# Block products of a recurrence summed two chunks at a time in 32x32 tiles of TensorE, with the projections issued in quarters

## The reference

```python
xa = _ln(x, ln1_w, ln1_b)
sx = shift(xa) - xa
mw, mk, mv, mr, mg = low-rank mixes of xa + sx * maa_x
w = exp(-exp(time_decay + tanh(xw @ decay_w1) @ decay_w2))
r, k, v = xr @ Wr.T, xk @ Wk.T, xv @ Wv.T        # 32 heads of 16
g = silu(xg @ Wg.T)
def step(s, inp):                                # s: 16 x 16 per head
    a = k_l[..., :, None] * v_l[..., None, :]
    out = einsum('bhs,bhst->bht', r_l, faaaa * a + s)
    return a + w_l[..., None] * s, out
y = group_norm(outs) * gn_w + gn_b
x = x + y * g @ Wo.T
rr = sigmoid(xr2 @ fWr.T); kk = square(relu(xk2 @ fWk.T))
x = x + rr * (kk @ fWv.T)
```

## Time and profile before

| | |
|---|---|
| median of 3 runs | 921.98 us (920.86 to 922.21) |
| profiled execution, its own time | 921.95 us |
| its span | 919.9 us |
| PE busy | 870.7 us, 6490 records |
| DVE busy | 639.5 us |
| ACT busy | 352.8 us |
| POOL busy | 294.9 us |

### The profile page before, as it was taken

How to read it: one execution, slowest core, us unless ns; L and a number is a source line. 1 busy time by engine, 2 the same in 40 slices (tenths; PEclk the granted TensorE clock), 3 DMA queues, 4 the chain that set the end, 5 groups by cost and what they waited for, 6 DMA issues and landing times.

```text
span 919.9 us, 16352 instructions
## 1 busy us (share of the span) xinstructions
PE 870.7 (95%) x6490; PEld 585.2 (64%) x6490; DVE 639.5 (70%) x1110; ACT 352.8 (38%) x715; POOL 294.9 (32%) x281
## 2 busy tenths in 40 slices
PE   7699999799999999999998999999999999999997
PEld 5477568457764686557764676646865577457674
DVE  3357966898479836997379954898468965986341
ACT  1222145523553146423363243531464236316422
POOL 3033641374107520373105720175202730640000
PEclk9799999899999999999999999999999999999999
DMA  8820102000010001100021000200001000000010
GB/s 309 307 69 0 47 20 75 1 1 1 2 69 24 1 2 60 56 1 1 2 70 47 1 1 2 93 23 1 2 24 46 1 1 2 24 24 2 1 46 23
DMA packets 17020, 34.09 MB, mean 37 GB/s; under 512 B 2224, under 2 KB 3888, under 8 KB 16944
## 3 DMA queue, kind: packets, MB, share of 16 engines
q1 hardware_dynamic: 14048, 31.20, 9.5%
q10 hardware_dynamic: 2896, 1.84, 0.6%
HBM read 24.65 MB, written 8.39 MB: 36 GB/s over the span
## 4 chain that ended last, share of the span: by engine, by line
PE 65%; DVE 17%; issue 5%; POOL 5%; ACT 4%; DMA 2%; SPq 1%; DVEq 0%; POOLq 0%; ACTq 0%
PE PB L496 21%; PE PC L502 8%; PE CH L578 6%; PE PC L496 6%; POOL prod L1953 3%; PE CH L637 3%; PE CH L614 3%; PE PC L671 3%; PE PA L489 3%; DVE av L1550 2%; PE PB L371 2%; DVE RA L1520 2%; DMA sq_Wo<-in_square 2%; DVE xmix L1458 2%; DVE wprod L1505 2%
## 5 line engine op out<-in xcount | busy, mean ns | idle before, releaser
L1943 POOL TENSOR_TENSOR xmix<-xmix,xa 128x512 f32<-128x512 f32 x80 | 96.5, 1227 | 190.9 <-DVE xmix L1458 190.9
L578 PE MATMUL CH<-prod,ones 128*128 128x512 f32 x272 | 143.3, 627 | 14.6 <-DVE prod L1482 5.2
L1953 POOL TENSOR_TENSOR prod<-RA,K 128x512 f32<-128x512 f32 x112 | 132.3, 1196 | 68.2 <-DVE RA L1520 41.0
L1458 DVE SCALAR_TENSOR_TENSOR xmix<-PA,chan,sx 128x256 f32<-128x256 f32 x160 | 66.1, 475 | 47.9 <-PE PA L489 47.9
L578 PEld LDWEIGHTS CH<-prod,ones 128*128 128x128 f32 x272 | 47.2, 194 | 64.9 <-issue 35.9
L1550 DVE TENSOR_TENSOR av<-CH,vT 128x512 f32<-128x512 f32 x112 | 76.2, 681 | 14.2 <-PE CH L578 14.0
L1132 ACT ACTIVATE st<-av,half 32x512 f32<-32x512 f32 x64 | 74.6, 1166 | 20.9 <-DVE av L1595 19.5
L1556 DVE TENSOR_REDUCE yred<-av 128x64 f32<-128x512 f32 (+2 forms) x112 | 76.9, 686 | 3.9
L496 PE MATMUL PC<-sqb,sq_fWk 128*128 128x256 f32 x256 | 58.6, 383 | 2.4 <-DVE sqb L1674 2.4
L496 PE MATMUL PB<-xmix,sq_Wg 128*128 128x256 f32 x256 | 58.5, 382 | 0.0
L496 PE MATMUL PB<-xmix,sq_Wr 128*128 128x256 f32 x256 | 58.5, 383 | 0.0
(11 more groups left out here) (162 smaller groups left out, 1407.2 us busy)
## 6 DMA issues: line engine op xcount, KB each, us to landing
x<-x_rows SPq DMA_DIRECT2D x11, 512.0 KB, 3.3
x<-in_x SPq DMA_DIRECT2D x8, 512.0 KB, 3.9
x_rows<-x SPq DMA_DIRECT2D x8, 512.0 KB, 3.4
out_x<-x SPq DMA_DIRECT2D x8, 512.0 KB, 2.7
ctx_t<-in_ctx SPq DMA_DIRECT2D x5, 512.0 KB, 4.9
y<-in_ctx SPq DMA_DIRECT2D x3, 512.0 KB, 8.1
sq_Wk<-in_square SPq DMA_DIRECT2D x1, 1024.0 KB, 13.1
sq_Wv<-in_square SPq DMA_DIRECT2D x1, 1024.0 KB, 16.4
```

Of the source, the lines that this page charges most:

```text
L578: pe.matmul(CH[:, (g % 2) * CHUNK:(g % 2 + 1) * CHUNK], ones16[:], prod[:, g % 3, :], start=True, stop=True).then_inc(chunk_mm, 1)
L1458: i = dve.scalar_tensor_tensor(xmix[:, SLOT_OF[name], ct, :], PA[:, ct * L:(ct + 1) * L], vec("maa_" + name, ct), sx[:, ct, :], ALU.add, A ...
L1943: pool.tensor_tensor(m, m, xa[:, ct:ct + 2, 1:L + 1], ALU.add).then_inc(mix_ready, 1)
L1953: pool.tensor_tensor(by_pair(prod[:, g % 3, :], h), r, k, ALU.mult).then_inc(prod_pool, 1)
```

## The change

**Pairs of chunks in tiles.** The chunks are visited in pairs (`VISITS`: 0 and 1, then 2 alone, then 3 and 4, and so on to 15 and 16). `ones16` is zero outside its 32x32 blocks on the diagonal too, so a sum needs only tiles (q, q) of the array: 32 partitions in, 32 out. The new code runs the first chunk of a pair on the four tiles (q, q) and the second on the four tiles (q, q+1), so that its sums land one quadrant (32 partitions) further: eight matmuls of 512 columns instead of two. The lone chunk is cut in two halves of 256 columns for the two sets. Since the second chunk's sums are shifted, the values they are weighed with have to be shifted too: the columns of Wv are rolled by 32 for that half of the channels at the start (on the host, as a layout of the weights), and the turns of v and of the sum `yint` use an identity of 160 columns that shifts back. Chunks are renumbered so that the halves of a pair lie in different halves of the channels.

**Waits.** PE waits for both products of a pair and for all weighings of the pair before it. `prod` has four buffers instead of three. DVE does both weighings of a pair, then both reductions. `D` (block decays) moves from `yred` to `prod`, and ACT's `b_block_decay` waits for `wprod_ready` instead of `yint_ready`.

**Quarters and order.** `a_phi_g` comes in two parts, and `a_key`, `a_value`, `a_receptance`, `a_gate`, `c_wo`, `c_key`, `c_receptance` and `c_value` in four quarters. The lists of all five queues are written anew.

```diff
-    CHUNKS = [(0, c) for c in range(DIAG)] + [(h, c) for h in INTRA for c in range(h)]
+
+    CHUNKS = [(0, 0), (0, 1), (1, 0)] + [(h, c + two * h // 2) for h in INTRA[1:] for c in range(h // 2) for two in range(2)]
     N_CHUNKS = len(CHUNKS)
+    VISITS = [(0, 2), (2, 3)] + [(g, g + 2) for g in range(3, N_CHUNKS, 2)]
...
-        ident = sb("ident", [P, P])
+        ident = sb("ident", [P, P + 32])
...
-        D = [yred[:, 0:L], yred[:, L:2 * L], prod[:, 2, 0:L], prod[:, 2, L:2 * L]]
+        D = [prod[:, 2 + ct // 2, (ct % 2) * L:(ct % 2 + 1) * L] for ct in range(CT)]
...
+        def chunk_sums(g):
+
+            h, c = CHUNKS[g]
+            lo = CHUNK // 2 if h == 1 else CHUNK * (c // max(h // 2, 1))
+            return CH[:, lo:lo + CHUNK]
...
+            def turn_values(values, t):
+
+                for ct in range(CT):
+                    lo = 32 * (ct // 2)
+                    mm = pe.matmul(CH[:, t * C + ct * P:t * C + (ct + 1) * P], values[:, ct * L + t * P:ct * L + (t + 1) * P],
+                                   ident[:, lo:lo + P], start=(ct == 0), stop=False, is_transpose=True, skip_group_check=True)
+                return mm
...
+            def columns_tile(out, mt, w, rhs, signal):
                 for kt in range(CT):
+                    mm = pe.matmul(out[:, mt * L:(mt + 1) * L], w[:, kt, mt * P:(mt + 1) * P], rhs[:, kt, :],
+                                   start=(kt == 0), stop=(kt == CT - 1))
+                if mt % 2:
+                    mm.then_inc(signal, 1)
+
...
-                    if u == 0 and g == 0:
+                for begin, end in VISITS:
+                    if not lo <= begin < hi:
+                        continue
+                    if u == 0 and begin == 0:
                         pe.wait_ge(w_const, 32)
-                    if g in POOL_CHUNKS:
-                        pe.wait_ge(prod_pool, len(POOL_CHUNKS) * u + POOL_CHUNKS.index(g) + 1)
+                    if begin in POOL_CHUNKS:
+                        pe.wait_ge(prod_pool, len(POOL_CHUNKS) * u + POOL_CHUNKS.index(end - 1) + 1)
                     else:
-                        pe.wait_ge(prod_dve, len(DVE_CHUNKS) * u + DVE_CHUNKS.index(g) + 1)
-                    if g >= 2:
-                        pe.wait_ge(av_ready, N_CHUNKS * u + g - 1)
+                        pe.wait_ge(prod_dve, len(DVE_CHUNKS) * u + DVE_CHUNKS.index(end - 1) + 1)
+                    if begin:
+                        pe.wait_ge(av_ready, N_CHUNKS * u + begin)
                     elif u:
                         pe.wait_ge(yn_ready, TT * u)
-                    pe.matmul(CH[:, (g % 2) * CHUNK:(g % 2 + 1) * CHUNK], ones16[:], prod[:, g % 3, :],
-                              start=True, stop=True).then_inc(chunk_mm, 1)
+                    for q in range(4):
+                        for turn in range(2):
+                            rows, o = slice(32 * q, 32 * (q + 1)), 32 * ((q + turn) % 4)
+                            if end - begin == 2:
+                                g = begin + turn
+                                out, v = chunk_sums(g)[o:o + 32], prod[rows, g % 4, :]
+                            else:
+                                g, half_chunk = begin, slice(turn * CHUNK // 2, (turn + 1) * CHUNK // 2)
+                                out, v = chunk_sums(g)[o:o + 32, half_chunk], prod[rows, g % 4, half_chunk]
+                            mm = pe.matmul(out, ones16[rows, rows], v, start=True, stop=True)
+                            if q == 3 and (end - begin == 2 or turn):
+                                mm.then_inc(chunk_mm, 1)
...
-                act.wait_ge(yint_ready, len(INTRA) * (u + 1))
+                act.wait_ge(wprod_ready, 4 * (u + 1))
...
+            def b_reduce(u, g):
+                h, c = CHUNKS[g]
+                if h == 0:
+                    return
...
-                    if g == 1:
+                for begin, end in VISITS:
+                    if not lo <= begin < hi:
+                        continue
+                    if CHUNKS[begin][0] == 1:
                         b_wprod(u)
-                    nxt = g + 2
-                    if nxt < N_CHUNKS and CHUNKS[nxt][0] > 1 and CHUNKS[nxt - 1][0] != CHUNKS[nxt][0]:
-                        b_update_r(u, CHUNKS[nxt - 1][0])
-                    if nxt in DVE_CHUNKS:
-                        b_prod(u, nxt)
-                    if nxt == N_CHUNKS:
-                        b_update_r(u, 8)
-                    b_weigh(u, g)
+                    for nxt in range(begin + 2, end + 2):
+                        if nxt < N_CHUNKS and CHUNKS[nxt][0] > 1 and CHUNKS[nxt - 1][0] != CHUNKS[nxt][0]:
+                            b_update_r(u, CHUNKS[nxt - 1][0])
+                        if nxt in DVE_CHUNKS:
+                            b_prod(u, nxt)
+                        if nxt == N_CHUNKS:
+                            b_update_r(u, 8)
+                    for g in range(begin, end):
+                        b_weigh(u, g)
+                    for g in range(begin, end):
+                        b_reduce(u, g)
...
-                pool.wait_ge(chunk_mm, N_CHUNKS * u + g - 2)
+                if g == 3:
+                    pool.wait_ge(scanned, CT * u)
+                if u or g > 3:
+                    pool.wait_ge(chunk_mm, N_CHUNKS * u + g - 3)
...
+    wvT = np.ascontiguousarray(a1["Wv"].T)
+    wvT[:, C // 2:] = np.roll(wvT[:, C // 2:].reshape(C, 2, P), 32, axis=2).reshape(C, C // 2)
...
-        "ident": np.eye(P, dtype=np.float32),
+        "square": np.stack([wvT if n == "Wv" else a1[n].T for n in SQUARE]),
+        "ident": np.eye(P, dtype=np.float32)[:, np.arange(P + 32) % P],
```

625 lines of the change are left out of this document (341 added, 284 removed).

## The result

The changed kernel takes 911.81 us (median of four runs, 909.61 to 912.53) against 921.42 (920.24 to 922.21) in the same session: ratio 0.9893, 95% interval 0.9871 to 0.9915, so 1.1% faster. I had said 898, 2.6% faster. The time lies in the range of 880 to 923, and almost on rival (b), 912, but less than half of the forecast gain is there.

A forecast was written before the change was run, and what follows sets the result against it. PE was busy 95% of the span, but DVE was taken as full too in the chunk stretch. 921.95 less 27.3 of gains plus 3 for the clock gave 897.7, said as 898 us; whole range 880 to 923.

The forecast's parts named there:

- rival (b): Chunk stretches: two or three clock falls in each, or short DVE waits each visit, lose half the gain; 912 us; 18 in 100.
- The allowance: TensorE's clock: one fall of 1.7 us in each of seven chunk stretches, three quarters swallowed by PE's idle time; 3 us.
- the ends: Fill and drain: batch 1 gains 3.3; drain 7.0 less 0.7, batch 6 3.6, batch 7 0.8, tail 3.7 us.
- The pair of chunks: PE's tiled sums: 1.06 us a pair, 0.65 for the lone chunk; PE loses 6.6 us of work a batch.
- Rival (c): Tiled sums: row strips writing one bank of CH take turns, a pair takes 3.6 us; 1018 us; 6 in 100.
- Rivals (a): Whole kernel: PE is the bound throughout and all 53 us of saved work come through; 869 us; 7 in 100.
- (d): Chunk visits: PE can't prepare one while DVE weighs; DVE waits 1.2 us at each of eight; 948 us; 6 in 100.
- with what batch 0 gives: Fill: half of `a_gate` moves into batch 1's wait for DVE; first weighing 3.3 us earlier, batch 0's contribution included; bounds 0 and 7.
- Batch 7's chunks: Drain: PE and DVE both full there, as `c_shift` and two quarters of `c_key` come in; gain 0.8 us.
- Pair over 1.5: Sign on PE's chunk pairs: the prediction is wrong if a pair takes over 1.5 us; 1.06 expected.
- under 0.95: Sign on TensorE: the prediction is wrong if the granted clock is under 0.95 over a turn.
- The third: Sign on DVE: wrong if its waits for CH reach 4 us a turn; under 2 expected.

The follow-up runs named there:

- e7: e1 plus dummies in the fill (three) and the drain (three, three and four), ahead of mix products and pairs; 899.33 us, ratio 0.9765 to the kernel before.
- e1: The change plus eight unread full-array matmuls (dummies) on PE before the pair of chunks 3 and 4 in each steady turn; 900.90 us, ratio 0.9789.
- e10: e7 with the kernel before's start: output weights turned behind the first phi and g, their copy behind the first sums; 903.60 us, ratio 0.9798.
- e2: The change with VectorE's four decay-factor products moved behind the lone chunk's weighing and level sum; 901.26 us, ratio 0.9792.
- e4: The change with a quarter of the output product moved between the lone chunk and the pair 3 and 4 in steady turns; 902.86 us, ratio 0.9808.
- e11: e1 with three dummies instead of eight before the pair 3 and 4; 900.63 us, ratio 0.9771.
- e8: e7 with the second key-product quarter of the next batch put between the two turns of z in steady turns; 913.61 us, ratio 0.9899.
- e12: e7 with three of four decay products moved behind the lone chunk's level sum, and two dummies instead of eight before pair 3 and 4; 895.24 us.
- e3: The change's order, quarters and buffers, but sums made by the full array instead of tiles; 922.10 us, ratio 1.0008.

## Why the prediction was wrong

Where the time went, stretch by stretch, by the first weighings of the batches in each trace (before: 173.70, 595.31, 702.74, 788.02; the change: 172.34, 591.80, 695.56, 776.96; e7: 173.94, 586.29, 687.90, 768.31):

| stretch | forecast | the change | e7, clock up |
|---|---|---|---|
| start to batch 1 | -3.3 | -1.4 | +0.2 |
| four turns, to batch 5 | -9.6 | -2.2 | -9.3 |
| to batch 6 | -6.3 | -3.7 | -5.8 |
| to batch 7 | -3.6 | -3.9 | -4.9 |
| to the end | -4.5 | +0.3 | -2.9 |
| sum | -27.3 | -10.8 | -22.6 |

- **The failed step is the clock.** I wrote "I allow one such fall in each of seven chunk stretches; PE's own idle time swallows three quarters: 3 us". There is one fall in each, as I said, but in the steady turns of 6.8 to 10.2 us where the row that I priced shows 3.4 (0.76 over 7 us), and PE's idle time does not swallow it, since the fall begins at the end of that idle time (within 1.2 us of it), at the pair that VectorE needs next. With the falls gone from the steady turns the four turns gain 9.3 against a forecast of 9.6. The allowance should have been 11 us (911.8 less 900.9), where I had 3. That is close to rival (b), whose chance of 18% was too low, but not in its words: not two or three falls in a stretch, but one that is two or three times as long. Its price of 1.7 a stretch was about right (the steady turns lost 1.0 to 2.4 each). That its 912 was hit is in part luck, since it had the ends at their forecast.
- **How much of the miss that is.** The forecast without its clock term is 894.7, and e7, with the clock up, takes 899.3. So about 9 of the 13.8 us between 898 and 911.8 are the clock, and some 4.6 are the ends, below.
- **What made the wait long** is a smaller error of mine. I wrote of idle time "in pieces up to 2.8, most while DVE makes the block decays", with the durations of before. In the change these operations run beside POOL's first products of r*k: all of a batch took 4.3 us instead of 2.7, and the piece was 3.90.
- **The steady turn, apart from the clock, was right.** A turn has two parts that meet at the second turn of z on PE. From there to the next first weighing PE is dense and takes 77.55 in the change (300.95 to 378.50) and 77.55 in e1 (296.41 to 373.96). The first part is VectorE's: 29.91 in the change, 27.82 in e1. So the whole difference of 2.1 is in VectorE's part. Of my own steps: from the end of the read to the first pair 12.4 forecast, 12.55 measured (578.07 to 590.62); from the first weighing to the last pair 40.6 forecast, 42.2 in the change (484.89 to 527.13) and 41.2 in e1 (479.35 to 520.54); from the last pair to the end of the next second read 50.6 forecast, 50.94 measured.
- **The pair of chunks** takes 1.02 against 1.06. Rival (c), 3.6 a pair and 1018 us, is refuted. The Trainium skill (TensorEngine Tiling (Array Packing), Restrictions and Gotchas) states that different row tiles can't access one PSUM bank at the same time; here four diagonal tiles of four row strips write one bank side by side, so the rule doesn't hold for tiles that write different partitions, and the measurement decides.
- **Rivals (a) and (d)** are out. PE isn't the bound throughout: in e1 it is idle for 3.8 us of a turn and does 3.4 of empty work. VectorE's waits of 1.2 at each of eight visits did not come either: with the clock up it waits 0.83 us for the first sums and 0.63 and 1.59 at the last two pairs, behind PE's dense quarters of keys, and at none in the middle.
- **Two of my own sums were off.** Rival (d)'s 9.6 a turn, eight times, is 77 us and not 50, which gives 975; and by (c)'s terms, (6.5 + 3.4) / 8 on 1.06, the change turns slower from 2.3 us a pair, not 2.4. Neither moves the forecast or its range.
- **The ends** are the rest, and only partly settled. The fill: half of `a_gate` did move into VectorE's wait, and from batch 0's first weighing to batch 1's it takes 4.5 less (89.04 for 93.54). But in batch 0 half of `a_gate` now stands ahead of the first pair too (78.58 to 82.12 on PE), and that batch's first weighing came 3.1 later (83.30 for 80.16), which my term "with what batch 0 gives" left out. The late `setup` isn't the cause (e10). Batch 7's chunks, from the first weighing to the turn of k, I forecast 0.8 shorter and they were 2.7 longer, in e7 1.0 longer, and the tail to the turn of y was 2.5 shorter, in e7 3.9, for a forecast of 3.7. So about 1.7 of batch 7's miss goes away with the dummies, and the rest is order in the drain, which no run took apart. The 1.5 by which the tails differ is mostly an idle time of 1.33 us of PE within `b_sums` (at 834.10) for which the profile shows no releaser; e1 and e7 don't have it, e2 has 1.03 there, and its cause is open.
- **My signs.** "Pair over 1.5" did not trip (1.02), and the clock over a turn is 0.95 to 0.97, at the edge of "under 0.95". The third did: VectorE's waits for CH add up to 5.55, 4.24 and 4.49 us in the three turns shown, over the 4 that I had named and far from the "under 2" that I expected; in e1 they are 3.05. First weighings were 106.4 to 107.5 apart and not 105.0; from the read to the first weighing it is 13.73 for 13.8.

## What to carry to other kernels

Price a change that shortens matmuls together with the wait it leaves. What a fall of the clock costs depends on whether the full engine runs out of work meanwhile: at the first pair behind the wait it cost 1.0 to 2.4 us a turn here, nothing where VectorE had work in hand (e2, e4, e11), and 1.6 in front of a dense stretch of PE (e8). A few empty full-array matmuls in that wait cost no time and gave 11 us here; real work moved into it gave at most 9, and 5 to 19 us less than the empty work where it put something else late. Durations of VectorE that were read where GpSimd was idle don't hold where a new order puts the two side by side.

## What the runs showed of the hardware

- **The clock falls behind a wait of PE of 2 to 4 us in the chunk stretch**, at the wait or a group or two behind it: in all five steady turns of the change (waits of 3.2 to 3.9), in three of e2 (2.7), two of e4 (2.0) and of e11 (2.4), one of e12 (2.0) and none of e1 (at most 1.5). It needs no tiles: with sums by the full array on both sides of a wait of 3.1 us, e3 has a fall in four of five. Nor does it need one long wait: in batch 6 of the change it fell behind two of 1.26 and 1.51 us with one mix step between them. Before the change PE waited less than 1 us at this place. The Trainium skill (TensorE: Matmul & The Clock Gate, Part 1: The HAM clock gate) says that the clock halves when the engine is idle; the rows agree in kind, 1.89 for 1.02 on the same pair. That dummies of 1.3 us had nearly the effect of 3.4 I had not expected.
- **VectorE beside GpSimd.** Operations of VectorE whose inputs both lie in SBUF stretch from 292 to 1326 ns (128x128) and from 1.67 to 4.31 us (`c_shift`) beside POOL's products, while the weighings, with one input in PSUM, stay at 0.68 beside the same products. The Trainium skill (SBUF — State Buffer, "SBUF: two separate sides") states that such an operation and one of GpSimd that reads SBUF exclude each other on a shared port pair. The rows of the change agree: its two smaller decay products, shown together at 487.44, end at 488.81 and 490.20, right behind the operations of POOL that end at 488.53 and 490.05:

```profile
485.60 2.94 POOL L2060 TENSOR_TENSOR prod<-RA,K 128x512 f32<-128x512 f32 x2 [0.17 <-POOL K L2072]
488.76 1.29 POOL L2072 TENSOR_TENSOR K<-K,wprod 128x512 f32<-128x512 f32 x1 [0.23 <-POOL prod L2060]
```

- The same code in the fill had a fall in one execution and none in another, which moved batch 1 by 3.2 us; differences below that between two profiled runs should be read per stretch.
